# Cross attention on one core: groups of heads handled in pairs, with six score banks and a ring of two banks for everything else

## The reference

```python
# B=32, S=512, C=640, 20 heads of 32 columns, 77 context tokens of 1024
q = heads(x @ to_q_w)                       # (32, 20, 512, 32)
k = heads(ctx @ to_k_w); v = heads(ctx @ to_v_w)
p = softmax(q @ k.T / sqrt(32))             # (32, 20, 512, 77)
out = merge(p @ v) @ to_out_w + to_out_b + x
```

## Time and profile before

| | |
|---|---|
| three runs | 1776.91, 1778.78, 1778.90 us; median 1778.78 |
| profiled execution | 1775.92 us, its span 1774.1 us (1.8 us lie around the span) |
| PE busy | 1744.7 us, 98% of the span |
| DVE, ACT, POOL busy | 1286.8, 1051.6, 495.7 us (73, 59, 28%) |
| DMA | 355.72 MB, mean 201 GB/s |

### The profile page before, as it was taken

The page is one execution under the profiler, slowest core; times in us unless marked ns, Lnnn a source line. Parts: engine busy times, 40 slices in busy tenths (PEclk is TensorE's granted clock), DMA queues, the critical chain, the costliest instruction groups (busy, mean ns, idle before and its releaser), DMA issues.

```text
span 1774.1 us, 38360 instructions
## 1 busy us (share of the span) xinstructions
PE 1744.7 (98%) x13448; PEld 1358.5 (77%) x13448; DVE 1286.8 (73%) x2537; ACT 1051.6 (59%) x5597; POOL 495.7 (28%) x735
## 2 busy tenths in 40 slices
PE   7999999899999999999999999999999999999998
PEld 7999998577777777777777777777777777777776
DVE  5322123778888888888888888888888888888874
ACT  4322113666666666666666666666666666666662
POOL 0111112333222333333333233322323333332221
PEclk9999999999999999999999999999999999999999
DMA  9543213778888888888888888888888888888864
GB/s 219 165 115 102 63 46 104 194 204 224 226 229 227 214 224 229 227 219 226 223 226 222 223 223 225 226 219 223 229 224 219 225 220 223 223 233 216 227 196 119
DMA packets 311184, 355.72 MB, mean 201 GB/s; under 512 B 40284, under 2 KB 194867, under 8 KB 310991
## 3 DMA queue, kind: packets, MB, share of 16 engines
q1 hardware_dynamic: 240175, 299.35, 62.2%
q10 hardware_dynamic: 66528, 41.30, 10.8%
q0 software_dynamic: 4288, 12.62, 2.1%
HBM read 173.59 MB, written 179.60 MB: 199 GB/s over the span
## 4 chain that ended last, share of the span: by engine, by line
PE 95%; DVE 1%; DMA 1%; ACT 1%; SPq 1%; issue 0%; POOL 0%; DVEq 0%; ACTq 0%
PE p_queries L840 32%; PE p_fill L886 31%; PE p_scores L862 9%; PE p_values L874 9%; PE p_bank L422 8%; PE p_bank L405 6%; ACT probs L669 1%; DMA ctx_raw<-in_ctx 1%; DMA k_scratch<-kv_out 0%; SPq L220 0%; DVE wv_split L344 0%; DVE negmax L719 0%; SPq L226 0%; DVE x_t L760 0%; POOL probs L641 0%
## 5 line engine op out<-in xcount | busy, mean ns | idle before, releaser
L669 ACT ACTIVATE probs<-p_scores,negmax 128x77 f32<-128x77 f32 x2560 | 787.9, 361 | 315.6 <-DVE negmax L719 315.6
L641 POOL TENSOR_TENSOR probs<-probs,rsum 128x308 f32<-128x308 f32 x640 | 446.6, 700 | 1002.7 <-DVE rsum L725 1002.7
L669 ACT ACTIVATION_READ_ACCUMULATOR probs<-p_scores,negmax 128x1 f32 x2560 | 623.8, 244 | 0.0
L840 PE MATMUL p_queries<-x_t,wq_split 128*128 128x512 f32 x2400 | 590.4, 398 | 1.0 <-DVE x_t L760 1.0
L886 PE MATMUL p_fill<-o_t,wo_split 128*128 128x512 f32 x2400 | 573.4, 391 | 0.1
L886 PEld LDWEIGHTS p_fill<-o_t,wo_split 128*128 128x128 f32 x2400 | 447.9, 188 | 95.5 <-issue 1.2
L840 PEld LDWEIGHTS p_queries<-x_t,wq_split 128*128 128x128 f32 x2400 | 442.5, 189 | 99.3 <-DVE x_t L760 1.8
L735 DVE STREAM_TRANSPOSE turned<-probs 128x384 f32<-128x384 f32 x640 | 353.0, 552 | 39.5 <-POOL probs L641 39.2
L862 PEld LDWEIGHTS p_scores<-k_sb,q_t 32*128 32x128 f32 x5120 | 157.4, 186 | 140.2 <-issue 140.2
L719 DVE TENSOR_REDUCE negmax<-p_scores 128x16 f32<-128x1232 f32 x160 | 228.9, 1431 | 19.0 <-PE p_scores L862 17.2
L725 DVE RECIPROCAL rsum<-sums 128x4 f32<-128x4 f32 x640 | 109.0, 170 | 126.6 <-ACT probs L669 122.2
(11 more groups left out here) (34 smaller groups left out, 652.0 us busy)
## 6 DMA issues: line engine op xcount, KB each, us to landing
p_scratch<-turned SPq DMA_DIRECT2D x159, 768.0 KB, 6.0
probs_t<-p_scratch SPq DMA_DIRECT2D x318, 256.0 KB
out<-out_blocks SPq DMA_DIRECT2D x126, 320.0 KB, 5.6
x_raw<-in_x ACTq DMA_DIRECT2D x124, 320.0 KB, 4.3
probs_t<-p_scratch SPq DMA_DIRECT2D x159, 104.0 KB
ctx_raw<-in_ctx SPq DMA_DIRECT2D x32, 256.0 KB, 7.8
k_sb<-k_scratch SPq DMA_DIRECT2D x32, 192.5 KB, 5.1
v_sb<-v_scratch SPq DMA_DIRECT2D x159, 38.5 KB
```

The costliest lines, as they stand in the source:

```text
L641: nc.gpsimd.tensor_tensor(heads_of(t), heads_of(t), rsum[:, slot, t, :].unsqueeze(2).to_broadcast([P, HG, N_TXT]), ALU.mult).then_inc(prob ...
L669: last = nc.scalar.activation(heads_of(t)[:, h, :], s_bank[:, h, t * N_TXT:(t + 1) * N_TXT], ACT.Exp, bias=negmax[:, slot, t, h:h + 1], ac ...
L840: last = nc.tensor.matmul(q_bank[:, :], wq_s[:, w, c, g * P:(g + 1) * P], x_t[:, a, c, :], start=c == 0 and i == 0, stop=c == CC - 1 and i ...
```

## The change

Two groups, 2k and 2k+1, now form a phase k; five phases (two batches) form a round, 16 rounds in all. Each engine's list is written for the five phases of a round.

- PE does both value products (groups 2k-4 and 2k-3), then both groups' scores, then two query projections and two output projections in turn: V V S S Q O Q O.
- The scores have six banks (`score_place`). The first group's take the first 308 columns of banks 0 to 3; the second group's heads 0 and 1 take banks 4 and 5, its heads 2 and 3 the free columns of banks 0 to 3. The second group's tiles 2 and 3 are issued first; its tiles 0 and 1 wait for `s_done` of the first group.
- Queries, outputs, values and the late units share the other two banks in the order in which PE makes them (`ring`). Each waits in `clear_bank` for whatever read the product two places before it.
- The maxima come in three operations: one for the first group (1232 columns), one for heads 2 and 3 of the second (616), one for heads 0 and 1 (616, step H). The first exponential waits for two of them, the second group's for the third. All wait until both groups' scores are done.
- The low parts of two of the five chunks of x go from DVE to POOL (`L6 L8 L11 L13` in `POOL`).
- Each of SP's lists waits for the phase's value products, then issues the loads and the two reads of probabilities, then the two writes. Outputs are stored, and x loaded, four DMAs at a time. The last two groups (before: the last one) take their value product from `turned` directly.

```diff
+TENSOR = orders("V S Q2 O-8 Q3 O-7 F1 F2",
+                "V S O-8 Q2 O-7 F3 Q3",
+                "V S Q2 O-8 Q3 O-7",
+                "V S Q2 O-8 Q3 O-7",
+                "V S Q2 O-8 Q3 O-7")
+SCALAR = orders("U V S0 S1 S2 S3 S4 S5 S6 F1 S7 F2",
+                "U V S0 S1 S2 S3 S4 F3 X5 X6 X7 X8 X9 S5 S6 S7 D2",
+                "U V S0 S1 S2 S3 S4 S5 S6 S7",
+                "U V S0 S1 S2 S3 S4 S5 S6 S7 X10 X11 X12 X13",
+                "U V X14 S0 S1 S2 S3 S4 S5 S6 S7 D3")
+VECTOR = orders("P-9 U V M H Z-9 R0 R1 T0 R2 T1 Q2 R3 T2 R4 T3 P-8 R5 T4 Z-8 R6 T5 Y5 Q3 R7 T6 Y6 T7 Y7",
+                "P-7 U V M H Z-7 R0 Y8 R1 T0 P-6 R2 T1 Z-6 R3 T2 Y9 R4 T3 Q2 T4 L5 L7 L9 P-5 R5 R6 T5 R7 T6 Q3 T7",
+                "U V M H Z-5 R0 R1 T0 R2 T1 Q2 R3 T2 R4 T3 P-4 R5 T4 Z-4 R6 T5 Y10 Q3 R7 T6 Y11 T7",
+                "P-3 U V M H Z-3 R0 R1 T0 Y12 R2 T1 Q2 R3 T2 R4 T3 P-2 R5 T4 Z-2 R6 T5 Y13 Q3 R7 T6 L10 T7 L12",
+                "P-1 Z-1 U Y14 V M L14 H R0 R1 T0 R2 T1 Q2 R3 T2 R4 T3 P0 R5 T4 R6 T5 Q3 R7 T6 T7 Z0")
+POOL = orders("N0 N1 N2 N3 N4 N5 N6 N7 F1 F2",
+              "N0 N1 N2 N3 N4 L6 L8 N5 N6 N7 F3",
+              "N0 N1 N2 N3 N4 N5 N6 N7",
+              "N0 N1 N2 N3 N4 N5 N6 N7 L11 L13",
+              "N0 N1 N2 N3 N4 N5 N6 N7")
+SYNC = orders("A C1 B", "A G-2 B", "A B", "A C2 B", "A G-1 B")
+TENSOR_END = orders("O152 V156 V157 O153 E158 O154 E159 O155 O156 O157 O158 O159")[0]
...
+        def score_place(second, t, h):
+            if not second:
+                return h, t * N_TXT
+            if h < 2:
+                return HG + h, t * N_TXT
+            return 2 * (t // 2) + h - 2, (QT + t % 2) * N_TXT
...
+            def exps(n, t):
                 if t == 0:
+                    act.wait_ge(max_ready, 3 * (n // 2) + (3 if n % 2 else 2))
+                if n > 0:
+                    act.wait_ge(probs_turned, QT * (n - 1) + t + 1)
...
+            def first_maxima(k):
+                dve.wait_ge(s_done, 2 * k + 2)
+                nc.vector.tensor_reduce(neg_first[:, :, :],
+                                        s_bank[:, 0:HG, 0:QT * N_TXT].rearrange("p h (t k) -> p h t k", k=N_TXT),
+                                        AX.X, ALU.max, negate=True).then_inc(max_ready, 1)
+                nc.vector.tensor_reduce(neg_second[:, 2:HG, :].rearrange("p a (b t) -> p (a b) t", t=2),
+                                        s_bank[:, 0:HG, QT * N_TXT:(QT + 2) * N_TXT]
+                                        .rearrange("p h (t k) -> p h t k", k=N_TXT),
+                                        AX.X, ALU.max, negate=True).then_inc(max_ready, 1)
...
+            def clear_bank(kind, n):
+                i = place[kind, n]
...
+                was, earlier = ring[i - 2]
+                if was == "F":
+                    pe.wait_ge(project["unit_copied"], LATE + earlier + 1)
+                elif was == "Q":
+                    pe.wait_ge(q_ready, earlier + 1)
+                elif was == "O":
+                    pe.wait_ge(out_added, earlier + 1)
+                else:
+                    pe.wait_ge(ot_low, earlier + 1)
...
+            def scores(n):
...
+                if n > 0 and n % 2 == 0:
+                    pe.wait_ge(exp_done, QT * n)
...
+                for t in FIRST_HALF:
+                    score_tile(n, t)
+                if n % 2:
+                    pe.wait_ge(s_done, n)
+                    if in_halves:
+                        pe.wait_ge(q_ready, n + 1)
+                    pe.sem_inc(scores_clear, 1)
+                for t in SECOND_HALF:
+                    last = score_tile(n, t)
+                last.then_inc(s_done, 1)
...
+            for k in range(PHASES):
+                for kind, index in steps(SYNC, k):
+                    if kind == "A":
+                        if k >= 2:
+                            sp.wait_ge(pv_done, 2 * k - 2)
+                            for n in (2 * k + 1, 2 * k + 2):
+                                if n < END[0]:
+                                    load_v(n)
+                        if k >= 1:
+                            read_probs(2 * k - 2)
+                            read_probs(2 * k - 1)
...
+                    elif kind == "B":
+                        for n in (2 * k, 2 * k + 1):
+                            if n < END[0]:
+                                write_probs(n)
```

## The result

The changed kernel takes 1869.96 us (median of 4 runs, 1869.63 to 1872.80) against 1777.97: 1.052 times the time of before, 95% interval 1.0509 to 1.0535. Slower was forecast, but 1819, with 1850 as the end of the range. The profiled execution is 1869.8 us, its span 1868.0, against 1775.9 and 1774.1.

The account below looks back on a forecast made before the run. PE, busy 98%, was taken as the bound: its 17.68 us a phase against 18.16, plus waits, made five phases 93.22 against 90.80. With start and end the span was 1814.7, the time 1819 us, range 1774 to 1850.

Parts of the forecast that it names:

- PE's own sum: PE's work in a phase without waits: 17.68 us against 18.16 before, 36 us less over 75 phases.
- The common wait: In a phase, the third long unit waits 0.50 us for DVE's copy of queries, ready at 9.40 us.
- The low parts: Subtractions for x on DVE and POOL: 0.62 us each on DVE, about 1.15 on POOL; contention 6 us more.
- the main case: Whole kernel: waits of the ring and of DVE's order give 1819 us, own range 1800 to 1840; chance 0.56.
- The start: First groups: group 0's scores start at 295.4 us, group 8's at 364.6, against 292.91 and 362.21 before.
- That PE never waits: Rival for all phases: the query copy and additions come in time, a phase is 17.68 us, total 1748; chance 0.10.
- Late probabilities: Rival at the value products: reading takes 12 us, each phase waits 1.1 more, total 1900; chance 0.06.
- Only the common wait: Rival: query copy at 9.40 us, but additions never late and phase 1 like the others, total 1790; chance 0.12.
- no turn would be saved: Rival at the second group's scores: a step of 1.07 us, 0.17 a phase more, total 1832; chance 0.08.
- One sign: In the new profile, DVE was to be near 80% busy, against 73% before.

Follow-up runs that it names:

- run 4: Changed kernel with each of the three maxima taken over 8 of the 77 keys, most of the maxima left out: 1771.0 us.
- run 8: Changed kernel with low parts on DVE in odd batches and POOL in even ones, and DVE's and ACT's lists reordered: 1763.1 us, ratio 0.992.
- Run 6: Changed kernel with the copy of queries that the third long unit waits for put earlier in DVE's list, in four of five phases: 1897.2 us.
- run 1: Changed kernel with all five low parts of x on DVE, none on POOL: 1881.5 us, ratio 1.059.
- run 2: Changed kernel with all five low parts of x on POOL, none on DVE: 1856.3 us.
- run 3: Changed kernel with DVE's addition that frees the second value product's bank put ahead of other work in phases 0 and 3: 1833.8 us, ratio 1.032.
- run 7: Changed kernel with additions first as in run 3, low parts of odd batches all on DVE, of even ones all on POOL: 1848.2 us, ratio 1.040.
- run 9: Kernel of run 8 with phase 1's old lists on ACT and DVE (x's high parts and a query copy later): 1803.5 us.

## Why the prediction was right in kind and wrong in size

**PE's own sum: right.** 17.68 a phase was forecast, 17.73 and 17.69 measured in runs 4 and 8. Two scores steps took 1.95 (forecast 1.97).

**The common wait: right.** Q3 was put at 9.40 us from the scores and starts at 9.37 (1035.00 - 1025.63); phases 0 and 2 came out at 18.69 and 18.32 (18.71 and 18.25). Run 6 shows that the copy's place is what it waits for, run 4 that the way ahead of it is.

**The low parts: the step that failed.** The prediction took 0.62 us for one on DVE and 1.15 for one on POOL, and made contention "6 us more, inside the main case". Measured are 1.12 and 1.61 in the mean, against 0.70 and 1.28 with the other engine making none (runs 1 and 2). The rule of the Trainium skill that the prediction weighed (SBUF — State Buffer, "Who interferes with whom") says that two such instructions contend, and the traces agree: 1.27 to 1.76 us for a low part on DVE that meets one on POOL, against 0.65 to 0.69. The prediction applied it to L7 behind L8 alone, and put the wait there at 0.4. Measured, L7 waits 1.08, since L8 had itself been held up by L5, and L5 waits 0.65 for L6. So the three in phase 1 take 3.59 us and not 1.87. Q3 needs L5 first and starts at 13.63 and not 12.91. The phase ends with the copy of Q3, and ahead of that DVE's list has R5, T5, R7 and T6, all behind the low parts: with DVE through its low parts at +15.78 the phase is 20.26 long, in run 1 at +15.23 it is 19.72; 19.24 was forecast. In phase 3 L10 waits 0.29 and L12 0.59, so the addition starts at 17.84 and not 17.01: 19.63 and not 18.77. The two phases are 1.9 of the 1.98 us by which a round was missed, 26 of 27.7 us in 14 rounds. Phase 3 was never weighed, although the same pair of engines subtracts there just ahead of a date that PE waits for.

**The clock: not in the prediction,** which had no term for it. In the full rounds it cost 11.2 us: 2.5 or 2.6 in four of them, 1.0 in one. Runs 1 and 6 have 1.75 and 1.77 us of idle time between the value products ahead of phase 4, and the clock falls in 8 and 12 of 14 rounds; the changed kernel, with 1.18, in 5; run 3, with no wait there, in none. Waits of 0.69 to 0.71 us between the two value products after phase 1 (the changed kernel, runs 3 and 4) never brought it down. The length of the wait is not all: after phase 1 run 1 waits 1.07 us and the clock holds in every full round, runs 7 and 9 wait 1.06 to 1.11 and it falls in 6 of 14 each. What else decides stays open.

**The start.** Scores of group 0 at 299.28 and not 295.4: PE waited 2.15 us for the first batch's second chunk, which POOL makes, and the granted clock fell to 0.50 behind it (with that batch on DVE, run 8 has neither and starts them at 295.28). The next ten groups took 95.3 us and not 87.4. The clock fell three times there, in the thin phases 1 and 2, where PE has no outputs to project, and at the start of phase 4, behind a wait of 2.97 us: in phase 4 the scores and the unit behind them take 8.68 us (373.69 to 382.37) where they take 5.48 at full clock (1025.63 to 1031.11). Contention is not what makes these phases long: run 7, which has none, takes 94.8. How the 7.9 us divide further stays open. The start is 11.7 us together. From group 150 to group 158 it is 1.1 more than forecast, and from there to the end 1.5. Sum: 27.7 + 11.2 + 11.7 + 2.6 = 53.2, of the 53.3 us by which the span of 1868.0 exceeds the 1814.7 forecast.

**The rivals.** That PE never waits was held off by the way through maxima and copy, as argued, and is what a better order brings. Late probabilities did not come: the chain has 1% for DMA, and no value product of the full rounds waits for one. Only the common wait failed in phases 0, 1 and 3; run 3 brings phases 0 and 3 down to 18.30 and 18.39 with the additions in time. That no turn would be saved is refuted by two scores steps in 1.95. One sign was wrong: DVE was to be near 80% busy, and is 70%; its 1303.4 us would have been 72% of the forecast span too, so no sum stood behind the 80.

**The change itself** therefore does what it is for: 0.48 us of PE's work a pair, 17.69 against 18.16. It pays for that with banks that each wait for one copy or addition, and the order of DVE's list put two of those behind work that nobody waited for.

## What to carry to other kernels

When buffers are merged into a ring, each reader of the ring gets a date; write down for every step of the in-order engine who waits for it and until when, and put those with a date ahead of those without: the same work took 1870 or 1763 us, by the order of two lists and by which engine makes which low part. Price a step that is moved to another engine beside what runs there at the same time, not by its row alone. Judge one wait only with the next one: run 6 took away a true wait and lost 27 us.

## What the runs showed of the hardware that was not expected

- DVE and POOL, both subtracting 128x512 fp32 operands in SBUF, slow each other: 0.70 to 1.12 us and 1.28 to 1.61 in the mean. One by one a low part on DVE is 0.65 to 0.69 or up to 1.76, by how much of POOL's instruction is left when it starts; the surcharge is that rest less 0.1 to 0.15 us, whichever engine comes second. A normalisation on POOL (0.70 us) does it too: 0.94.
- The granted clock fell to 1.2 GHz behind waits of PE of 1.1 to 1.8 us between two value products, in some rounds and not in others of the same execution, and stayed there for some 3 or 7 us (10 in runs 1 and 6); a round lost 1.0 to 4.3 us by it (4.3 in run 6: 99.1 in place of 94.8). A wait of 1.17 us ahead of a projection, the third long unit of phase 1, never did that. What tells the two places apart was not tried.
